# Merging a transformer block's opening program block into its LN1 and V block on one Trainium2 core

## The reference

```
def _layernorm(x, axis=-1, eps=1e-05):
    m = jnp.mean(x, axis=axis, keepdims=True)
    v = jnp.var(x, axis=axis, keepdims=True)
    return (x - m) / jnp.sqrt(v + eps)

# _L0_attn_ref(h, Wq, Wk, Wv, Wo): q, k, v = h@Wq, h@Wk, h@Wv in 16 heads of 64; rotary on q and k;
#   causal softmax(q k^T / 8) v; then @ Wo
# _L0_ffn_ref(x, codes, scales): Wg, Wu, Wd = NF4[codes] * scales (blocks of 64), inner size 2752;
#   (silu(x Wg^T) * (x Wu^T)) Wd^T
x = L0_attn_hidden_states
x = x + _layernorm(_L0_attn_ref(_layernorm(x), Wq, Wk, Wv, Wo))
x = x + _layernorm(_L0_ffn_ref(_layernorm(x), gate, up, down codes and scales))
```

## Time and profile before

| | us |
|---|---|
| runs of the kernel before | 3293.02, 3297.59, 3301.31 (median 3297.59) |
| the profiled execution: own time | 3296.03 |
| its span in the trace | 3294.24 |
| PE busy | 2897.0 (88% of the span) |
| DVE busy | 2390.9 (73%) |
| ACT busy | 2022.5 (61%) |
| POOL busy | 121.6 (4%) |

### The profile page before, as it was taken

The page is one execution under the profiler, slowest core; times in us unless marked ns, Lnnn a source line. Parts: engine busy times, 40 slices in busy tenths (PEclk is TensorE's granted clock), DMA queues, the critical chain, the costliest instruction groups (busy, mean ns, idle before and its releaser), DMA issues. The chain is left out here.

```text
span 3294.2 us, 58839 instructions
## 1 busy us (share of the span) xinstructions
PE 2897.0 (88%) x17856; PEld 1547.4 (47%) x17856; DVE 2390.9 (73%) x4289; ACT 2022.5 (61%) x4003; POOL 121.6 (4%) x397
## 2 busy tenths in 40 slices
PE   4989999688888888985883699999999999999996
PEld 2534444466666666663441244444444444444442
DVE  6535555688888888884556787787777777777767
ACT  1114443688888888882214767676676676676742
POOL 0000000000000000000002000000000000000002
PEclk9999999899999999997996899999999999999998
DMA  4322222201010101102112111111111111111124
GB/s 164 116 77 58 76 76 64 72 22 40 22 41 22 40 22 35 27 5 86 64 70 69 53 52 49 50 52 52 46 52 49 50 52 45 53 46 52 52 71 153
DMA packets 77773, 188.88 MB, mean 57 GB/s; under 512 B 12304, under 2 KB 12688, under 8 KB 77200
## 3 DMA queue, kind: packets, MB, share of 16 engines
q1 hardware_dynamic: 77456, 185.13, 17.7%
HBM read 151.52 MB, written 33.55 MB: 56 GB/s over the span
## 5 line engine op out<-in xcount | busy, mean ns | idle before, releaser
L1234 PE MATMUL gp<-region,wgu 128*128 128x512 f16 x4224 | 931.3, 383 | 89.3 <-DVE wgu L1392 89.3
L1271 ACT ACTIVATE line<-code,offsets 128x512 f32<-128x512 f32 x1056 | 697.2, 713 | 111.3 <-DVE below L1370 45.7
L1234 PEld LDWEIGHTS gp<-region,wgu 128*128 128x128 f16 x4224 | 416.0, 99 | 600.9 <-issue 110.9
L786 ACT ACTIVATE probs<-logits,nbias,coef 128x512 f32<-128x512 f32 (+3 forms) x640 | 461.0, 720 | 100.4 <-POOL nbias L719 86.4
L1247 PE MATMUL yp<-wd,inter 128*128 128x512 f16 x2112 | 463.9, 380 | 24.5 <-DVE wd L1392 17.4
L835 DVE SCALAR_TENSOR_TENSOR pt_pair<-tp,pt_pair 128x512 f16<-128x512 f32 (+3 forms) x640 | 385.8, 603 | 76.2 <-ACT pt_pair L795 72.4
L736 PE MATMUL logits<-k_sb,q_sb 128*128 128x512 f16 (+3 forms) x1280 | 347.3, 354 | 104.6 <-ACT probs L786 61.2
L819 DVE TENSOR_REDUCE mx<-logits 128x1 f32<-128x512 f32 (+3 forms) x640 | 383.9, 600 | 33.7 <-PE logits L736 33.1
L795 ACT ACTIVATE pt_pair<-tp 128x512 f16<-128x512 f32 (+3 forms) x640 | 343.4, 537 | 25.2 <-PE tp L749 21.0
L749 PE MATMUL tp<-ident,probs 128*128 128x128 f32 x2176 | 349.2, 276 | 4.3 <-DVE pt_pair L835 2.7
L548 PE MATMUL pq<-region,wt_pair 128*128 128x512 f16 x1536 | 333.4, 380 | 14.9 <-DVE wt_pair L599 14.9
(11 more groups left out here) (107 smaller groups left out, 2823.0 us busy)
## 6 DMA issues: line engine op xcount, KB each, us to landing
qk_pairs<-r_pair SPq DMA_DIRECT2D x128, 128.0 KB, 2.1
k_sb<-qk_pairs SPq DMA_DIRECT2D x64, 256.0 KB, 5.4
cst<-in_gate_codes SPq DMA_DIRECT2D x44, 256.0 KB, 2.6
sst<-in_gate_scales SPq DMA_DIRECT2D x88, 128.0 KB, 2.9
cst<-in_up_codes SPq DMA_DIRECT2D x44, 256.0 KB, 2.7
sst<-in_up_scales SPq DMA_DIRECT2D x88, 128.0 KB, 3.1
cst<-in_down_codes SPq DMA_DIRECT2D x44, 256.0 KB, 2.7
sst<-in_down_scales SPq DMA_DIRECT2D x88, 128.0 KB, 3.0
```

What stands on the lines that cost most here:

```text
L786: a.activation(probs[:, g0 % P_RING, 0:w * P], sp_[:, g0 % S_RING, 0:w * P], ACT.Exp, bias=nbias[:, m:m + 1], scale=col(coef, 0), accum_ou ...
L1234: mm = pe.matmul(gp[:, e % 2, m, :], wgu[:, par, m, a, col0:col0 + P], xnT[:, b, k, tok], start=(k == 0 and a == b), stop=(k == KT - 1 and ...
L1271: a.activation(line[:, k % 4, :], code7[:, :], ACT.Identity, scale=slope, bias=offsets[:, k:k + 1]).then_inc(s_L.sem, 1)
```

## The change

The opening block is gone and its work stands inside the LN1 and V block.

- SP loads x tile 0 first, then parts 0 to 3 of Wv, x tile 1, parts 4 to 7, then the first two sets of Wq, Wk and Wo parts, then the `flat` arrays; the loop begins at tile 2.
- DVE does rows(0), the maxima of parts 0 to 3, rows(1), lo(0), the maxima of parts 4 to 7, `powers` for Wv alone, the eight low parts of Wv, then what was passed over: the weight maxima of tiles 0 and 1, the clearing of `sums` and the maxima of `flat`. Then comes the loop, as before.
- ACT writes the high part of tile 0 and then the eight high parts of Wv before its loop.
- PE runs tiles 0 and 1 outside its loop; in the first half of projection 0 it waits for each part k of Wv in turn (`s_wvlo`) and so can begin with the first.
- POOL does `inverse_root` of tiles 0 and 1 before the maximum over partitions for Wv; the loop begins with tile 2.
- Gate, up and down are joined to Wq, Wk and Wo in the last maximum over partitions, and their `powers` and products stand at the end of the block.

```diff
-                v.memset(sums[:, :, :, :], 0.0).then_inc(chain.sem, chain.one())
...
+                rows(0, 0)
+                for k in range(KT):
+                    sp.dma_start(wv_f32[:, k, :], wv_v[:, k, :]).then_inc(d_wv.sems[k], 16)
+                    if k == 3:
+                        rows(1, 1)
+                for u in range(2):
+                    weights(u, u)
+                for m in range(3):
+                    sp.dma_start(flat[:, m, :], scales_flat[m]).then_inc(d_flat.sems[0], 16)
+                with sp.Fori(1, ST // 2) as it:
                     for u in range(2):
-                        step(it * 2 + u, it, u)
+                        rows(it * 2 + u, u)
+                        weights(it * 2 + u, u)
...
+                            if first and n == 0:
+                                pe.wait_ge(s_wvlo.sem, s_wvlo.done(k))
...
+                pe.wait_ge(s_id.sem, s_id.done(4))
                 transposes(0, 0)
-                with pe.Fori(0, ST // 2 - 1) as it:
+                for u in range(2):
+                    transposes(u + 1, 1 - u)
+                    project(u, u, u == 0)
+                with pe.Fori(1, ST // 2 - 1) as it:
...
                 hi(0, 0)
+                a.wait_ge(s_facv.sem, s_facv.done(0))
+                for k in range(KT):
+                    a.activation(wv_pair[:, 0, k, :], wv_f32[:, k, :], ACT.Copy,
+                                 scale=col(wfac, V_)).then_inc(s_wvhi.sem, 1)
...
+                v.tensor_copy(ident_bf[:, :], ident[:, :]).then_inc(first.sem, first.one())
+                v.tensor_copy(mask_bf[:, :], mask_f32[:, :]).then_inc(first.sem, first.one())
                 rows(0, 0, 0)
+                for k in range(4):
...
                 rows(1, 0, 1)
                 lo(0, 0)
+                for k in range(4, KT):
...
+                v.tensor_reduce(col(absmax, V_), vmax[:, :], AX_X, ALU.max).then_inc(s_maxv.sem, 1)
+                v.wait_ge(s_allv.sem, s_allv.done(0))
+                powers(v, first, V_, V_ + 1)
+                v.sem_inc(s_facv.sem, 1)
+                for k in range(KT):
+                    v.wait_ge(s_wvhi.sem, s_wvhi.done(k))
...
+                                           op1=ALU.subtract).then_inc(s_wvlo.sem, 1)
+                for u in range(2):
+                    weights(u, 0, u)
+                v.memset(sums[:, :, :, :], 0.0).then_inc(first.sem, first.one())
+                v.wait_ge(d_flat.sems[0], d_flat.done(0))
+                for m, c in enumerate((G_, U_, D_)):
...
-                powers(v, chain, Q_, O_ + 1)
+                powers(v, chain, Q_, D_ + 1)
                 product(v, chain, 0, [Q_, K_], 2.0 ** -11)
                 product(v, chain, 1, [V_, O_], 2.0 ** -18)
+                product(v, chain, 2, [G_], 2.0 ** -24)
+                product(v, chain, 4, [G_, U_, D_], 2.0 ** -7)
+                v.wait_ge(chain.sem, chain.at)
+                v.tensor_scalar(col(coef, 3), col(wfac, G_), 2.0 ** -45, None,
+                                ALU.mult).then_inc(chain.sem, chain.one())
...
+                for u in range(2):
+                    pool.wait_ge(s_var1.sem, s_var1.done(u))
+                    inverse_root(pool, st1[:, u, :], s_eps1, s_root1, u)
+                pool.wait_ge(s_maxv.sem, s_maxv.done(0))
+                pool.partition_all_reduce(allmax[:, V_:V_ + 1], absmax[:, V_:V_ + 1], P,
+                                          bass.bass_isa.ReduceOp.max).then_inc(s_allv.sem, 1)
+                with pool.Fori(1, ST // 2) as it:
```

More of the change, by code:

```diff
@@ L190, in build @@
         sums = sb("sums", [P, ST, HEADS, SC], F32, c04)
-        Q_, K_, O_, V_, G_, U_, D_ = range(7)
+        Q_, K_, O_, G_, U_, D_, V_ = range(7)
         def col(t, n):
@@ L311, in build @@
         c1 = ctx.enter_context(ExitStack())
+        flat = sb("flat", [P, 3, I * E // BLOCK // P], F32, c1)
+        vmax = sb("vmax", [P, KT], F32, c1)
         xt = sb("xt", [P, 2, E], F32, c1)
@@ L343, in _, with rows @@
             def _(sp):
-                def step(i, it, u):
+                def rows(i, u):
                     sp.wait_ge(s_h.sem, s_h.room(i))
@@ L411, in _, with weights @@
                     v.sem_inc(s.sem, s.credit)
[L413 to L417, removed]
+                def weights(i, it, u):
                     v.wait_ge(d_ws.sems[u], d_ws.done(it))
@@ L422, in rows @@
                     mx.then_inc(s_wm.sem, 1)
+                def rows(i, it, u, between=None):
+                    chain = Count(s_c1, i * CHAIN1)
+                    v.wait_ge(d_x.sems[u], d_x.done(it))
+                    layernorm_stats(v, chain, (xt[:, u, 0:CH], xt[:, u, CH:E]), st1[:, u, :], s_var1)
+                    if between:
+                        between(i, it, u)
                     v.wait_ge(s_root1.sem, s_root1.done(i))
@@ L441, in v_lo @@
                         op0=ALU.mult, op1=ALU.subtract).then_inc(s_vlo.sem, 1)
+                first = Count(s_c0)
+                v.wait_ge(s_id.sem, s_id.done(5))
+                v.tensor_copy(ident_bf[:, :], ident[:, :]).then_inc(first.sem, first.one())
+                v.tensor_copy(mask_bf[:, :], mask_f32[:, :]).then_inc(first.sem, first.one())
                 rows(0, 0, 0)
+                for k in range(4):
+                    v.wait_ge(d_wv.sems[k], d_wv.done(0))
+                    v.tensor_reduce(col(vmax, k), wv_f32[:, k, :], AX_X, ALU.max,
+                                    apply_absolute_value=True).then_inc(first.sem, first.one())
@@ L444, in _ @@
                 rows(1, 0, 1)
                 lo(0, 0)
+                for k in range(4, KT):
+                    v.wait_ge(d_wv.sems[k], d_wv.done(0))
+                    v.tensor_reduce(col(vmax, k), wv_f32[:, k, :], AX_X, ALU.max,
+                                    apply_absolute_value=True).then_inc(first.sem, first.one())
+                v.wait_ge(first.sem, first.at)
+                v.tensor_reduce(col(absmax, V_), vmax[:, :], AX_X, ALU.max).then_inc(s_maxv.sem, 1)
+                v.wait_ge(s_allv.sem, s_allv.done(0))
@@ L446, in _ @@
+                v.memset(sums[:, :, :, :], 0.0).then_inc(first.sem, first.one())
+                v.wait_ge(d_flat.sems[0], d_flat.done(0))
+                for m, c in enumerate((G_, U_, D_)):
+                    v.tensor_reduce(col(absmax, c), flat[:, m, :], AX_X, ALU.max,
+                                    apply_absolute_value=True).then_inc(first.sem, first.one())
+                v.wait_ge(first.sem, first.at)
                 with v.Fori(0, ST // 2 - 1) as it:
                     for u in range(2):
-                        rows(it * 2 + u + 2, it + 1, u)
+                        rows(it * 2 + u + 2, it + 1, u, weights)
```

29 lines of the change are left out of this document (24 added, 5 removed).

## The result

| | median us | range, runs |
|---|---|---|
| before, all its runs beside the changed kernel | 3295.63 | 3292.76 to 3301.31, 20 |
| after | 3304.54 | 3298.79 to 3308.04, 20 |
| ratio | 1.0026 | 95% interval 1.0019 to 1.0033 |

What follows compares the result with a forecast made beforehand. PE was taken as the bound from the second projection on, its start hanging on DVE's work on Wv. Second projection −13.2 us, `coef` +0.9, sum −12.3 against the median 3297.59: forecast 3285 us, range 3279 to 3292.

Steps and rivals of the forecast that it cites:

- the end of the sum: Whole kernel: second projection 13.2 us earlier, `coef` instructions at the block's end +0.9, so 12.3 us gained.
- the train: PE's projections from the second on: PE always busy, so everything behind gains what the train's start gains.
- Steps 1 to 5: DVE's head, from x tile 0's load to Wv's last maximum: `ht` of tile 0 at 8.2 us, maxima until 22.1.
- Step 6: Join, maximum over partitions, `wfac`, Wv's low parts: until 34.5 us, with 0.3 us added for POOL's code switch.
- the other switch: POOL's code switch at 31.5 us before the first L303 in the old trace: 8.2 us from switch to run.
- the sign of 0.9 us from DVE's join: Check in the changed profile: POOL's maximum over partitions runs within 0.9 us of DVE's join.
- The sentence with the bounds: POOL's switch for the maximum over partitions: takes anything up to 16.1 us; with 7.3 us cover, costs 0 to 8.8.
- Step 8: DVE's rows(2), first turn of the loop: 4.43 us from the start of statistics to the end of `ht`, until 44.7.
- T: Time when `ht` of tile 2 is ready for PE: 45.0 us.
- PE behind it: PE after projection 0: idle about 4 us, fallen clock costing 1.7, projection 1 ends at 58.1 us, 13.2 earlier.
- the rival of POOL's code paid at the call: POOL's switches in the head, paid at the call: +4.0 us, so −8.3 in all, 3289; chance 0.16.
- The slower rival: POOL's code late twice in the head, root(0) 8.2 us and maximum over partitions 8.8 − 0.3: +4.4, 3302; chance 0.05.

Runs made afterwards that it cites:

- e7: e1 with both x tiles loaded first, both roots before all eight maxima and lo(0) behind `wfac`: 3284.72 us, ratio 0.9963 to the kernel before.
- e1: The changed kernel with 30 semaphore increments that nobody waits for, near the start of PE's stream: 3288.16 us, ratio 0.9973 to the kernel before.
- e9: The changed kernel with 30 increments on PE behind the attention loop, at the head of attention's output: 3303.02 us, ratio 1.0014 to the kernel before.
- e5: The changed kernel with 29 semaphore increments near the start of PE's stream: 3297.72 us, ratio 1.0003 to the kernel before.
- e6: The changed kernel with 28 semaphore increments near the start of PE's stream: 3324.03 us in a single run.
- e3: The changed kernel with tiles 0 and 1 back in PE's loop, waits for Wv's parts in each pass: 3299.49 us, ratio 1.0008 to the kernel before.
- e2: The kernel before with 226 more PE instructions in its opening block (224 increments, two branches): 3319.63 us, ratio 1.0069 to the kernel before.

## Why the prediction was wrong

- **The step that failed is the end of the sum**, "−13.2 + 0.9 = −12.3 us", by way of the sentence that the train's earlier end is what everything behind gains. All behind the block was taken to be as it was. Its instructions were; their place in PE's code was not. The attention loop gave back 13.6 us, more than the head had gained. No rival had this mechanism: all of them, the slower one too, looked for the loss in the first 60 us. The trace of before did have the signs, six waits of 16.7 us in all "<- issue" at the loop's seams and 141 packets of 16 KB code, and I read none of them, since the change seemed to end at 232 us. The comparison of instruction order, which the prediction used for DVE and POOL, would have shown the longer code on PE.
- **Steps 1 to 5 held.** `ht` of tile 0 ended at 7.98 (8.2 forecast), the last Wv maximum at 21.6 (22.1).
- **Step 6, POOL's switch, was mis-sized: 0.3 taken, 2.7 measured.** The maximum ran at 24.64, 2.8 us after its release, where 0.14 was usual (17.86 to 18.00 before), and 9.7 us from the switch at 14.9; the term went by the 8.2 of the other switch as if a load had one length. The 2.8 broke the sign of 0.9 us from DVE's join. The sentence with the bounds had covered it (0 to 16.1). The mechanism, a load that runs from the switch on whatever POOL waits for, is borne out by e7, where the wait ended 10.3 us after the switch and the instruction ran at once. The Trainium skill, in "GPSIMD Engine Reference", section 2.1, has 5.95 us for it, with the wait subtracted; the two loads here took 8.2 and 9.7 with the wait inside. Less the wait they cost 2.6 and 2.8, so the page's figure doesn't fit either.
- **Step 8** was 0.4 short. So T was 47.6 for 45.0.
- **PE behind it.** It waited 4.92 us (4 forecast), the clock fell, and the transposes and projection 1 took 61.66 − 47.69 = 13.97 us for the forecast 13.1, so the second projection ended 9.7 us earlier, not 13.2. The train kept that (its last output ends 9.7 us earlier), the weight parts of tile 2 were not late, and the `coef` instructions cost the forecast 0.9: Q and K began 8.8 us earlier.
- **The size of the head alone** can be read from e1: 8.4 us in the medians (in its profiled execution Q and K begin 9.3 earlier, 233.3 for 242.6). The forecast for it was 12.3; the rival of POOL's code paid at the call was at 8.3, which is chance, since e7 refutes its mechanism.
- **The slower rival** stood at 3302, near the measured 3304.5, by luck: its first part, a late root of tile 0, didn't occur (`ht` of tile 0 ended at 7.98), and the second cost 2.7 us, not 8.8.

## What to carry to other kernels

When a change unrolls, adds or removes instructions on an engine, look at every long loop that stands behind it in that engine's stream, touched or not: waits "<- issue" at its seams and the packets of the instruction queue tell whether it fetches code each turn. If so, measure the change with a few no-ops ahead of the loop (here 30, at no cost that e1 or e9 shows), or a good change is taken for a bad one: e1 and e5 lie 0.3% apart with one no-op between them. And a switch of POOL's code cost nothing here where some 10 us of other work stood between it and its first use, and 2.7 us where there were 7.

## What the runs showed of the hardware

- Code placement alone moved this kernel by 36 us: 3288.16 with 30 no-ops, 3297.72 with 29, 3324.03 with 28 (one run).
- A seam of the attention loop at which one fetch is waited for cost 2.4 to 3.0 us; in e6, with two, it was 5.3 to 6.25. In e3, e5 and e6 a seam of the FFN loop cost 3.1 to 4.4.
- PE's code of a loop of 2245 instructions was fetched again each turn (77 packets of 16 KB), that of a loop of 396 was not (one packet in eight turns).
- In the changed kernel more of the loss came from the clock than from the stalls: the "issue" waits grew by 4.9 us (15.2 + 6.4 − 16.7) and PE's busy time by 10.9. In e9 it was 8.4 and 7.3. In the four kernels whose attention loop has the longer stalls (the changed kernel, e2, e6, e9) the clock fell at all six seams, for 31 to 38 us in all; in the other seven at two or three, with 7 to 14 us in the loop.
- POOL's code load took 8.2 us in one case and 9.7 in another, counted from the switch, and overlaps with POOL's wait.
